# Key rotation of a four-layer kernel: ScalarE exchanges the halves, VectorE multiplies twice, and four rotations move one block ahead

## What is computed

```
def _L2_ffn_ref(x, W_base, b_base, W_router, lora_A, lora_B):      # layer 2, feed-forward
    probs = softmax(x @ W_router.T); topk_p, topk_i = top_k(probs, 2); w = weights of the two experts
    lora_out = einsum('ter,eor,te->to', einsum('td,erd->ter', xf, lora_A), lora_B, w) * 2.0
    return x @ W_base.T + b_base + lora_out

def _rotate_half(x):                                               # layer 3, attention
    x1, x2 = jnp.split(x, 2, axis=-1)
    return jnp.concatenate([-x2, x1], axis=-1)

k = (key @ wk) ...;  k = k * cos + _rotate_half(k) * sin           # 8 key heads of 128
q = (query @ wq) ...; q = q * cos + _rotate_half(q) * sin          # 32 query heads
attn = softmax(q @ k.T / sqrt(128) + mask);  out = (attn @ v) @ wo
```

## Time and profile before

| | |
|---|---|
| median of 3 runs | 1869.63 us (1868.19 to 1872.62) |
| profiled execution | 1867.98 us, of which the span of the core is 1866.0 us |
| mean granted TensorE clock | 0.99 of full speed |
| feed-forward block of layer 2 | about 1255 to 1315 us |
| norm block of layer 3 | about 1315 to 1327 us |
| opening of layer 3 (to the end of the second head's first steps) | about 1327 to 1371 us |

### The profile page before, as it was taken

How to read it: one execution, slowest core, us unless ns; L and a number is a source line. 1 busy time by engine, 2 the same in 40 slices (tenths; PEclk the granted TensorE clock), 3 DMA queues, 4 the chain that set the end, 5 groups by cost and what they waited for, 6 DMA issues and landing times. The chain is left out here.

```text
span 1866.0 us, 29554 instructions
## 1 busy us (share of the span) xinstructions
PE 1785.1 (96%) x10312; PEld 1504.8 (81%) x10312; DVE 1413.0 (76%) x2854; ACT 650.9 (35%) x1783; POOL 672.5 (36%) x453
## 2 busy tenths in 40 slices
PE   7999999999999999996998998879999999999998
PEld 5788899889888889985876665665888888888886
DVE  7677777777777777765546877779788888888886
ACT  4422232233332123214025665531343433343333
POOL 5533433344443343314241003425443343333331
PEclk9999999999999999998999998989999999999999
DMA  4111111011111111101010002010111111011011
GB/s 172 61 51 51 36 36 48 32 51 51 51 51 51 51 39 32 34 12 65 23 45 20 1 26 64 28 62 1 46 35 35 34 34 34 34 34 34 34 35 46
DMA packets 32026, 78.27 MB, mean 42 GB/s; under 512 B 4096, under 2 KB 10944, under 8 KB 31584
## 3 DMA queue, kind: packets, MB, share of 16 engines
q1 hardware_dynamic: 31968, 77.50, 12.6%
HBM read 75.39 MB, written 2.10 MB: 42 GB/s over the span
## 5 line engine op out<-in xcount | busy, mean ns | idle before, releaser
L657 POOL TENSOR_TENSOR l0x_comb<-l0x_neg,l0x_bias 128x1024 f32<-128x1024 bf16 x32 | 69.2, 2161 | 377.2 <-DVE l0x_probs L1058 362.8
L952 ACT ACTIVATE l0x_probs_t<-bank 128x512 f32<-128x512 f32 x32 | 19.1, 596 | 503.0 <-PE bank L794 503.0
L2891 POOL TENSOR_TENSOR l3x_q<-l3x_q,l3x_cross 128x512 f32<-128x512 f32 x64 | 89.8, 1408 | 187.9 <-DVE l3x_q L1862 187.9
L39 PE MATMUL bank<-l0x_w_v_hi,ctx_lo 128*128 128x256 f32 x512 | 144.9, 283 | 0.0
L37 PE MATMUL bank<-l0x_w_v_hi,ctx_hi 128*128 128x256 f32 x512 | 144.9, 283 | 0.0
L38 PE MATMUL bank<-l0x_w_v_lo,ctx_hi 128*128 128x256 f32 x512 | 144.9, 283 | 0.0
L936 ACT ACTIVATE l0x_probs<-l0x_probs,l0x_top 128x129 f32<-128x129 f32 x256 | 99.4, 390 | 53.9 <-DVE l0x_top L1062 53.9
L3078 ACT ACTIVATE l3x_probs<-l3x_probs,l3x_top 128x128 f32<-128x128 f32 x256 | 99.1, 388 | 38.2 <-DVE l3x_top L3159 38.1
L37 PE MATMUL bank<-ctx_hi,l0x_w_k_hi 128*128 128x512 f32 x256 | 103.7, 405 | 7.8 <-DVE ctx_lo L1140 7.8
L1102 DVE TENSOR_TENSOR x<-x,bank 128x512 f32<-128x512 f32 x120 | 82.1, 684 | 37.5 <-PE bank L39 37.5
L37 PE MATMUL bank<-l3x_qin_hi,l3x_w_q_hi 128*128 128x512 f32 x256 | 105.1, 411 | 2.2 <-ACT l3x_v L3112 1.9
(11 more groups left out here) (488 smaller groups left out, 5328.2 us busy)
## 6 DMA issues: line engine op xcount, KB each, us to landing
l0x_raw_k<-L_k_dram SPq DMA_DIRECT2D x32, 256.0 KB, 3.3
l0x_raw_v<-L_v_dram SPq DMA_DIRECT2D x16, 512.0 KB, 3.3
l0x_raw_q<-L_q_dram SPq DMA_DIRECT2D x16, 512.0 KB, 4.3
l0x_raw_o<-L_o_dram SPq DMA_DIRECT2D x16, 512.0 KB, 3.3
l3x_raw<-L_q_dram SPq DMA_DIRECT2D x16, 512.0 KB, 3.2
l3x_raw<-L_o_dram SPq DMA_DIRECT2D x16, 512.0 KB, 3.2
kv_raw<-L_kv_dram SPq DMA_DIRECT2D x8, 512.0 KB, 3.3
l0x_ctx_raw<-ctx_t_dram SPq DMA_DIRECT2D x4, 512.0 KB, 5.7
```

The source lines that it names most:

```text
L39: return pe.matmul(out, lhs[1], rhs[0], start=False, stop=stop)
L657: pool.tensor_tensor(comb[:, :, :], neg[:, :, :], bias[:, j:j + 1, :].to_broadcast([P, B, P]), ALU.add).then_inc(comb_ready, 1)
L952: act.activation(probs_t[:, 0:BH, :], bank[6][:, :].rearrange("p (b n) -> p b n", b=BH), ACT.Copy).then_inc(t_act, 1)
L2891: pool.tensor_tensor(dst[:, part], dst[:, part], cross[n][:, :], ALU.add).then_inc(rotated, 1)
```

## The change

`rotate` loses its two sine operations of 64 partitions and gets one multiplication of 128 partitions in place of them, with a third table that holds the sine with the signs for exchanged halves. The exchange itself becomes a method `swap` on ScalarE: two copies of 64 partitions for each key unit. The waits on the drained unit and on the join of unit u - 2 go from VectorE to ScalarE; VectorE waits for the swap. The third table makes one transfer at 1101 us a half larger than it was (3 rows of 128 floats for each partition in place of 2).

Of the five rotations in the last layer's opening four are moved into the feed-forward block: the loop over the batches now rotates ahead of each batch, not from the third on, and two rotations stand behind the last batch. GpSimd joins 15 units in that block and 1 in the last layer.

```
     def rotate(self, dve, count):
         for u in range(self.turned, self.turned + count):
             part, cross = self.key_part(u), self.cross[u % 2][:, :]
             if u == 0:
                 dve.wait_ge(self.rope_loaded, 16)
-            dve.wait_ge(self.drained, u + 1)
-            wait(dve, self.k_joined, u - 1)
-            sine_products(dve, self.rope, part, cross).then_inc(self.sines, 1)
-            dve.wait_ge(self.sines, u + 1)
+            dve.wait_ge(self.swapped, u + 1)
+            dve.tensor_tensor(by_batch(cross), by_batch(cross), self.rope[:, 2:3, :].to_broadcast([P, BH, P]), ALU.mult)
             cosine_product(dve, self.rope, part, part).then_inc(self.cosines, 1)
         self.turned += count
+
+    def swap(self, act, count):
+
+        low, high = slice(0, P // 2), slice(P // 2, P)
+        for u in range(self.exchanged, self.exchanged + count):
+            part, cross = self.key_part(u), self.cross[u % 2]
+            act.wait_ge(self.drained, u + 1)
+            wait(act, self.k_joined, u - 1)
+            act.activation(cross[high, :], part[low, :], ACT.Copy)
+            act.activation(cross[low, :], part[high, :], ACT.Copy).then_inc(self.swapped, 1)
+        self.exchanged += count
...
                 if ahead:
                     ahead.low(pool, 10)
-                    ahead.join(pool, 11)
+                    ahead.join(pool, 15)
...
             def _(act):
                 if ahead:
+                    ahead.swap(act, 2)
                     ahead.high(act, 10)
...
                 if ahead:
                     ahead.drain(act, 5)
+                    ahead.swap(act, 2)
                     ahead.drain(act, 2)
                 for half in range(2):
                     act.wait_ge(t_full, half + 1)
                     act.activation(ht[:, half * HALF:(half + 1) * HALF], bank[half][:, :], ACT.Copy).then_inc(t_done, 1)
                 if ahead:
+                    ahead.swap(act, 11)
                     ahead.drain(act, 3)
...
                 for b in range(B):
-                    if ahead and b >= 2:
+                    if ahead:
                         ahead.rotate(dve, 1)
                     dve.wait_ge(o_full, b + 1)
...
                         core.statistics(dve, b)
+                if ahead:
+                    ahead.rotate(dve, 2)
...
         def first_high(act):
+            ahead.swap(act, 1)
             ahead.drain(act, 3)
```

More of the change, by code:

```diff
@@ L1741, in __init__ @@
         self.made, self.copied, self.turned, self.joined = 0, 0, 0, 0
-        self.rope_loaded, self.sines, self.cosines = core.sem("kv_rope_loaded"), core.sem("kv_sines"), core.sem("kv_cosines")
+        self.exchanged = 0
+        self.rope_loaded, self.swapped, self.cosines = core.sem("kv_rope_loaded"), core.sem("kv_swapped"), core.sem("kv_cosines")
         self.k_joined = core.sem("kv_joined")
@@ L2894, in _ @@
                 rotate_both(0, q[0])
-                ahead.join(pool, 1)
                 split_low(1, w_q[1])
                 def turn(g, first, last):
-                    if first:
-                        ahead.join(pool, 1)
                     rotate_both(ring_at(g, "q1"), q[1])
-                    if first:
-                        ahead.join(pool, 2)
                     if not last:
@@ L2976, in _ @@
                 ahead.multiply(pe, 3)
-                pe.wait_ge(ahead.k_joined, 11)
+                pe.wait_ge(ahead.k_joined, 15)
                 def step(g, j, needed, at, bk, w, n_w, project_next, weigh_last, units=0):
@@ L3199, in _ @@
                     rotate(n, 0, 0, 0, q[0], 0)
-                ahead.rotate(dve, 1)
                 dve.wait_ge(mask_loaded, 16)
@@ L3207, in step @@
                         copy_probs(h - 1)
-                    else:
-                        ahead.rotate(dve, 1)
                     if rotate_next:
@@ L3222, in turn @@
                     if first:
-                        ahead.rotate(dve, 2)
                         dve.wait_ge(ahead.k_joined, 2 * GROUPS)
```

5 lines of the change are left out of this document (3 added, 2 removed).

## The result

The changed kernel takes 1873.98 us (median of 9 runs, 1872.17 to 1876.55), the kernel before 1869.0 us beside it (9 runs, 1867.15 to 1874.38). The ratio is 1.0023, interval 1.0014 to 1.0031: 2.6 to 5.8 us slower, an interval that holds both likely outcomes of the prediction, slower and (up to 3.7 us) no change to be told. The profiled execution took 1873.67 us, with a span of 1871.7.

A forecast was written before the change was run, and what follows sets the result against it. TensorE was taken to bound the kernel, VectorE mattering only where TensorE waits. -0.95 + 3.35 + 1.8 - 1.89 = +2.3 us, plus 1.7 for the clock, gave 1869.63 + 4.0 = 1873.6 us; range 1868.6 to 1876.6.

The forecast's parts named there:

- one fall of the clock: Case: TensorE's clock falls once, behind the pause before `base_product(3)`; 1873.6 us, chance 0.33.
- The start: Feed-forward block's start: first rotations finish 1.5 us earlier, so TensorE's wait behind a ScalarE drain goes; -0.95 us.
- The dearer copies of the rival: Rival: exchange copies on ScalarE take 0.81 us or more, about 1874.3 us; chance 0.12, shared with an unseen wait.
- The first addition: Batch 0's addition to x: unit 4's exchange queues behind the copies of h, so TensorE waits before `base_product(3)`; +3.35 us.
- The batches behind: Later batches: VectorE needs under 2.9 us each against TensorE's step of 4.3 us, so no further wait.
- The block's end: Feed-forward block's end: two rotations and a join behind the last statistics delay the barrier; +1.8 us.
- The last layer: Last layer's opening: four rotations leave VectorE, so TensorE's wait for ScalarE's copy of the values goes; -1.89 us.
- The norm block: Norm block behind the feed-forward block: the exchange there, 1.15 us ahead of a ScalarE drain, costs nothing.
- The clock: Behind the new 3.35 us pause: one fall, sized from 4.90 us at 0.65 behind a 3.12 us pause; +1.7 us.

The follow-up runs named there:

- e1: Changed kernel with the exchanges of units 4 and 5 put ahead of ScalarE's copies of h; 1869.83 us, ratio 0.9995 to the kernel before.
- e5: e1 with the two rotations behind the last batch put ahead of batches 5 and 6 instead; 1868.63 us, ratio 0.9988 to the kernel before.
- e7: Kernel before without the rotations and joins of units 12 to 15, waits lowered to 12; 1867.43 us, ratio 0.9986.
- e2: Changed kernel plus three spare TensorE products, results unused, ahead of `base_product(3)`; 1873.47 us, ratio 1.0011 to the kernel before.
- e4: Changed kernel with the rotations back where the kernel before has them, exchange kept on ScalarE; 1870.45 us, ratio 0.9996.
- e6: Kernel before with the ScalarE exchange for units 0 and 1 only, and the third table; 1869.37 us, ratio 1.0002.
- e3: Kernel before with four rotations moved into the feed-forward block, all of three VectorE operations, no exchange; 1877.71 us, ratio 1.0045.

## Why the prediction was right

It gave 1873.6 us for 1873.98, and its likeliest case, one fall of the clock, is the one that came. That the number is met within 0.4 us is partly luck: it forecast +4.0 us over a median of 1869.63, and it became 4.98 over one of 1869.0, or 4.59 in the marks, in which a clock term that was too small by 1.1 us was partly covered by others. The mechanism is what was right. Term by term:

- **The start, -0.95 predicted, -1.19 measured.** TensorE's wait for the drain is gone and the transposes of h come 1.18 to 1.19 us earlier in every kernel with the exchange. VectorE comes to the router's copies 2.2 us earlier and not 1.5 (1263.60 - 1256.35 against 1264.70 - 1255.24), which gains nothing more. The dearer copies of the rival did not come: this is the answer on the tile `kv_cross` (line, duration in ns least/median/most, starts).

```profile
L1845 ACT ACTIVATE kv_cross<-kv_keys x16: 627/628/632, 1256.3 to 1322.9; 64x512 f32<-64x512 f32 x16
```

- **The first addition, +3.35 predicted, +3.55 measured.** The chain was as written: copies of h, exchange of unit 4, rotation 4, rotation 5 against the join, addition. e1 shows the cause by moving it away. The +0.2 is what three small errors leave: an exchange takes 1.27 us (0.63 + 0.64) and not 1.15, TensorE starts 0.82 us behind the start of the addition (1290.90, 1291.72) and not 0.68, and against these the first operation of a rotation blocks the second for 0.61 us and not 0.69.
- **The batches behind, no wait predicted, none found.** TensorE has no bracket from `base_product(3)` to the block's end.
- **The block's end, +1.8 predicted, +1.59 measured.** The pause is 2.48 us and the clock stayed up behind it. GpSimd's last join ends at 1322.47, after VectorE (1321.13) and ScalarE's last drain (1320.91), and TensorE goes on 0.5 us later:

```profile
1321.21 1.26 POOL L1853 TENSOR_TENSOR kv_keys<-kv_keys,kv_cross 128x512 f32<-128x512 f32 x1 [0.63 <-DVE kv_keys L1872]
```

  e5 shows that the loss came from the two rotations that stood last.
- **The last layer, -1.89 predicted, -2.27 measured.** The mechanism was right: e7 gains the same 2.27. The term was too small because I took the bracket for the whole price. A bracket is counted from the modelled end of the last product before it, while products in a stream start closer together than they are long (0.28 us long, 0.12 apart in the value units), and the first product behind a pause holds up the next a little longer. TensorE in the kernel before, at the wait and some us behind it:

```profile
1359.21 0.39 PE L38 MATMUL bank<-l3x_qin_lo,l3x_w_q_hi 128*128 128x512 f32 x1
1359.44 0.40 PE L39 MATMUL bank<-l3x_qin_hi,l3x_w_q_lo 128*128 128x512 f32 x1
...
1361.73 0.28 PE L37 MATMUL bank<-kv_w_hi,kv_ctx_hi 128*128 128x256 f32 x1
1361.85 0.28 PE L38 MATMUL bank<-kv_w_lo,kv_ctx_hi 128*128 128x256 f32 x1
```

  The product that waited began at 1358.88, 0.33 us ahead of the next, and that one 0.23 ahead of the third. So the wait cost about 1.89 + (0.28 - 0.12) + 0.10 = 2.15 us; the last 0.1 is not located. The same difference stands in the pause above, where 3.38 us in brackets moved the mark by 3.55.
- **The norm block, 0 predicted, +0.16 measured.** The exchange of unit 15 stands in this block, and TensorE's wait for `l3x_qin_lo` is 1.19 us there (row at 1331.33) where it was 1.05. The other kernels with an exchange in this place (e1, e2, e4, e5) show 0.14 to 0.16 more from mark to mark, e6 and e7, which have none, show nothing more, and e3, which has none either, has the wait of 1.05 us. No run moved this exchange alone.
- **The clock, +1.7 predicted, +2.85 measured.** This is the term that was mis-sized, by 1.1 us. The pause of 3.38 us was indeed followed by a fall and that of 2.48 was not, as taken. But I sized the fall by the stretch behind one other pause, 4.90 us at 0.65, which is 3.4 us at 1.2 GHz (4.90 x 0.35 x 2). Here it was 6.7 us (6.80 x 0.49 x 2), and TensorE worked in 5.6 of them. e2 measures the same term by filling the pause: 4.59 - 1.73 = 2.86 us.

The sum was off by +0.6 (4.6 for 4.0), since the clock's +1.1 was partly covered by -0.6 from the start and the last layer. The marks' 4.59 lies inside the 2.6 to 5.8 us of the measured interval. The spans differ by 5.7 us, but 1.1 of these lie ahead of the router's product, where the kernels differ only in one transfer and where the executions scatter by 5 us.

Open is what decides whether the clock falls behind a pause of 1.9 us, and how often it does in the kernel before. The 11 runs of e7, which has no such pause, had a mean granted clock of 0.988, and the 21 of the kernel before beside them 0.987; that is a hint that it does in some, not more. And the shares of the term in e4 and e6 rest on one profiled execution each; their intervals hold no change as well as a gain.

## What to carry to other kernels

When work goes to an engine that is mostly idle, look at what stands ahead of it in that engine's queue, not at its busy share: ScalarE is 36% busy, and two exchanges placed behind two copies cost 6.4 us between two profiled executions (after against e1), of which 2.9 came from the clock. Such an exchange is cheap if it is issued at the last point where ScalarE waits anyway. Work that is moved to the end of a block with a barrier is paid there as far as no other engine covers it (4.9 us of rotations and join, from 1317.56 to 1322.47, cost 1.6), while the same work between two batches that TensorE paces cost nothing (e5). Where a pause of TensorE can't be avoided, useless products in it kept the clock up and were worth 2.9 us in the profiled execution here.

## What the runs showed of the hardware

The length of a pause alone did not decide the clock. Behind pauses of 2.48 us (after), 2.42 us (e3) and 1.89 us (before) it stayed at 1.00; behind 1.90 us (e6) it was 0.67 over the next 5.2 us, with 3.38 us (after) 0.51 over 6.8 us, and behind 5.95 us (e3) 0.55 over 5.2 us. Nor did the fall come when TensorE resumed: in the changed kernel it came 2.2 us into the pause, and in e6 about 0.6 us after its end (0.70 from 1358.00 to 1359.00, 0.50 over the next us). What a fall costs varied as well: 1.7 us with 3.12 us of pause, 2.85 us with 3.38 us. The Trainium skill, TensorE: Matmul & The Clock Gate, section What's actually happening, has it that only two clocks are granted. The windows fit that, read as mixtures of 0.5 and 1.

A ScalarE copy of 64 partitions from one half of SBUF to the other took 0.628 us, a straight one of 128 partitions 0.622: crossing over with half the partitions changed the price by 1%. No run has a crossing and the number of partitions apart. The second copy of an exchange starts 0.64 us after the first (1285.95, 1286.59), so the two don't overlap.
